# Full attention on one core: another order for TensorE inside each quarter of a head

## The reference, cut to what matters

```python
q = (hidden_states @ Wq.T + bq).reshape(b, s, HEADS, HEAD_DIM)
k = (hidden_states @ Wk.T + bk).reshape(b, s, HEADS, HEAD_DIM)
v = (hidden_states @ Wv.T + bv).reshape(b, s, HEADS, HEAD_DIM)
q = q * SCALE
scores = jnp.einsum('bqhd,bkhd->bhqk', q, k)
probs = jax.nn.softmax(scores.astype(jnp.float32), axis=-1).astype(scores.dtype)
out = jnp.einsum('bhqk,bkhd->bqhd', probs, v).reshape(b, s, d)
```

## Time and profile before

| | us |
|---|---|
| median of 3 runs (lowest to highest) | 3234.82 (3233.41 to 3235.3) |
| the profiled execution's own time | 3234.58 |
| its span, first to last instruction | 3232.9 |
| mean granted TensorE clock over the span | 0.934 |
| PE busy / DVE busy / ACT busy | 2513.5 / 2434.3 / 1832.9 |

### The profile page before, as it was taken

The page is one execution under the profiler, slowest core; times in us unless marked ns, Lnnn a source line. Parts: engine busy times, 40 slices in busy tenths (PEclk is TensorE's granted clock), DMA queues, the critical chain, the costliest instruction groups (busy, mean ns, idle before and its releaser), DMA issues. The chain is left out here.

```text
span 3232.9 us, 47502 instructions
## 1 busy us (share of the span) xinstructions
PE 2513.5 (78%) x12729; PEld 1044.9 (32%) x12911; DVE 2434.3 (75%) x4025; ACT 1832.9 (57%) x3590; POOL 1223.4 (38%) x1651
## 2 busy tenths in 40 slices
PE   5797799999999698799999999696745555555575
PEld 4543222222222443233333333284521010101454
DVE  6667788888886566777777777264279999999833
ACT  1212588888888111255555555303239999999521
POOL 1014533333331213378888888703550000000154
PEclk9899899999999699899999999887979999999688
DMA  3001322222221302712222222352131111110012
GB/s 94 1 1 62 100 79 71 78 71 78 71 79 54 95 1 77 252 61 80 81 83 77 73 80 68 107 211 60 40 109 40 33 32 32 33 33 26 18 45 81
DMA packets 192110, 223.46 MB, mean 69 GB/s; under 512 B 55152, under 2 KB 120944, under 8 KB 191472
## 3 DMA queue, kind: packets, MB, share of 16 engines
q1 hardware_dynamic: 152256, 192.41, 18.4%
q0 software_dynamic: 29696, 23.27, 3.1%
q10 hardware_dynamic: 9968, 5.51, 0.6%
HBM read 136.67 MB, written 83.76 MB: 68 GB/s over the span
## 5 line engine op out<-in xcount | busy, mean ns | idle before, releaser
L1253 DVE TENSOR_REDUCE neg_max<-ps 128x1 f32<-128x1024 f32 x512 | 602.5, 1219 | 93.8 <-PE ps L1147 87.0
L1632 POOL TENSOR_TENSOR acc<-acc,prob 128x512 f32<-128x512 f32 (+3 forms) x640 | 577.8, 943 | 87.5 <-PE ps L1481 87.5
L1226 ACT ACTIVATE prob<-ps 128x512 f32<-128x512 f32 x1024 | 556.3, 601 | 88.1 <-PE ps L1161 74.8
L2071 DVE TENSOR_REDUCE neg_max<-ps 128x1 f32<-128x1024 f32 x512 | 579.3, 1210 | 3.2 <-PE ps L2057 3.2
L2093 ACT ACTIVATE ps<-ps,neg_max 128x1024 f32<-128x1024 f32 x512 | 557.2, 1088 | 0.3 <-DVE neg_max L2071 0.3
L2057 PE MATMUL ps<-k_stack,q_stack 128*128 128x512 bf16 x992 | 303.5, 386 | 277.1 <-ACT ps L2093 273.9
L1561 ACT ACTIVATE prob<-ps 128x512 f32<-128x512 f32 (+3 forms) x640 | 266.5, 477 | 247.9 <-PE ps L1465 122.1
L1602 DVE TENSOR_REDUCE neg_max<-ps 128x1 f32<-128x128 f32 (+7 forms) x512 | 388.0, 758 | 17.5
L1161 PE MATMUL ps<-q_stack,k_stack 128*128 128x512 bf16 x946 | 292.8, 386 | 6.8 <-ACT prob L1226 4.6
L1171 PE MATMUL ps<-prob,v 128*32 128x512 f32 x2048 | 280.9, 620 | 3.7 <-ACT prob L1226 0.7
L1600 DVE TENSOR_TENSOR ps<-ps,mask_qk 128x128 f32<-128x128 f32 x512 | 151.1, 295 | 148.3 <-PE ps L1438 144.8
(11 more groups left out here) (304 smaller groups left out, 3820.0 us busy)
## 6 DMA issues: line engine op xcount, KB each, us to landing
q_stack<-q_parts SPq DMA_DIRECT2D x576, 48.0 KB
k_stack<-k_parts SPq DMA_DIRECT2D x576, 48.0 KB
o_quads<-o_out SPq DMA_DIRECT2D x64, 256.0 KB
v<-v_wide SPq DMA_DIRECT2D x32, 512.0 KB
o_pairs<-o_out SPq DMA_DIRECT2D x64, 256.0 KB, 6.2
num<-o_pairs SPq DMA_DIRECT2D x8, 2048.0 KB
q_parts<-parts SPq DMA_DIRECT2D x24, 384.0 KB, 2.7
k_parts<-parts SPq DMA_DIRECT2D x24, 384.0 KB, 2.7
```

The costliest lines, as they stand in the source:

```text
L1226: nc.scalar.activation(prob[:, m % RING, :], ps[:, bank(m), :], ACT.Exp).then_inc(exped.sem, 1)
L1253: nc.vector.tensor_reduce(neg_max[:, i.slot(2), m:m + 1], ps[:, first:first + 2, :].rearrange("p b n -> p (b n)"), AX.X, ALU.max, negate=T ...
L1632: nc.gpsimd.tensor_tensor(sums, sums, weights(j, u, h), ALU.add).then_inc(added.sem, 1)
L2071: nc.vector.tensor_reduce(neg_max[:, i.slot(2), qt:qt + 1], ps[:, 2 * (qt % 4):2 * (qt % 4) + 2, :], AX.XY, ALU.max, negate=True).then_inc ...
```

## The change

The order of TensorE in each group becomes: first pass `2g`, second score `4g`, first pass `2g + 1`, second scores `4g + 1` and `4g + 2`, prob by v of the group before, second score `4g + 3`. The transpose of the maxima moves from the end of group 1 to group 0, between prob by v and the last second score, and ACT's copy of it from behind the eighth exponential to behind the third. The rotation of banks is written as a list of 17 turns for each head; since 17 is no multiple of 3, a head starts on another bank than the one before it, where before each head started on bank 4. The waits for banks follow from that list.

```diff
-    TURN = NT // 2
+    turns = [0, 1, 2, "max"] + list(range(3, NT))
...
+    def bank(what, c):
+
+        return S2 + (len(turns) * c + turns.index(what)) % RING2
+
+    def wait_for_bank(pe, what, c):
+
+        at = len(turns) * c + turns.index(what) - RING2
+        while at >= -len(turns):
+            j, user = divmod(at, len(turns))
+            user = turns[user]
+            if user == "max" and 0 <= j + 1 < HEADS:
+                m_read.wait(pe, j + 1)
+                return
+            if user != "max" and 0 <= j < HEADS:
+                exped.wait(pe, j * NT + user)
+                return
+            at -= RING2
...
                 for g in range(4):
+                    if one:
+                        first_pass(i, 2 * g)
                     if two:
-                        for m in range(4 * g, 4 * g + 3):
-                            second_scores(j, m, there(n, 1))
+                        second_scores(j, 4 * g)
+                    if one:
+                        first_pass(i, 2 * g + 1)
+                    if two:
+                        second_scores(j, 4 * g + 1)
+                        second_scores(j, 4 * g + 2)
                     if g > 0 and two:
                         weigh(j, g - 1)
                     if g == 0 and there(n, 3):
                         weigh(i - 3, 3)
+                    if g == 0 and there(n, 1):
+                        turn_shift(i - 1)
                     if two:
-                        second_scores(j, 4 * g + 3, there(n, 1))
-                    if one:
-                        first_pass(i, 2 * g)
-                        first_pass(i, 2 * g + 1)
-                    if g == 1 and there(n, 1):
-                        turn_shift(i - 1, j if two else None)
+                        second_scores(j, 4 * g + 3)
...
-                    if g == 0 and there(n, 3):
+                    if m == 3 and there(n, 3):
                         read_output(i - 3, n)
-                    if g == 1 and there(n, 1):
+                    if m == 2 and there(n, 1):
                         h = i - 1
                         m_mm.wait(act, h.times(1))
```

More of the change, by code:

```diff
@@ L1148, in first_pass, with second_scores @@
                                  k_low[i.slot(2)][low, :], start=True, stop=True).then_inc(s1_mm.sem, 1)
-            def second_scores(j, n, turned):
+            def second_scores(j, n):
                 kt, c = tiles[n]
[L1153 to L1161, removed]
+                wait_for_bank(pe, n, j.c)
+                nc.tensor.matmul(ps[:, bank(n, j.c), :], ks[j.slot(4)][:, kt * P:(kt + 1) * P],
                                  qs[j.slot(4)][:, c * GROUP:(c + 1) * GROUP], start=True,
@@ L1172, in weigh, with turn_shift @@
                                      start=kt < 2, stop=kt >= KTS - 2).then_inc(pv_mm.sem, 1)
-            def turn_shift(h, j):
+            def turn_shift(h):
                 split.wait(pe, h.times(1))
                 m_read.wait(pe, h.times(1, -1))
-                if j is not None:
-                    exped.wait(pe, j.times(NT, TURN - RING2))
-                nc.tensor.transpose(ps[0:SHIFT * KTS, MAX_BANK, 0:P // 2].bitcast(BF16),
+                wait_for_bank(pe, "max", h.c - 1)
+                nc.tensor.transpose(ps[0:SHIFT * KTS, bank("max", h.c - 1), 0:P // 2].bitcast(BF16),
                                     shift[:, h.slot(2), :], S.ident_b[:]).then_inc(m_mm.sem, 1)
@@ L1220, in step @@
                 j = i - 2
[L1221 to L1227, removed]
-                    if g == 0 and there(n, 3):
+                for m in range(NT):
+                    if there(n, 2):
+                        s2_mm.wait(act, j.times(NT, m))
+                        pv_mm.wait(act, j.times(NT, m - RING))
+                        nc.scalar.activation(prob[:, m % RING, :], ps[:, bank(m, j.c), :],
+                                             ACT.Exp).then_inc(exped.sem, 1)
+                    if m == 3 and there(n, 3):
                         read_output(i - 3, n)
-                    if g == 1 and there(n, 1):
+                    if m == 2 and there(n, 1):
                         h = i - 1
@@ L1236, in step @@
                         nc.scalar.activation(shift_rows[0:SHIFT * KTS, h.slot(2), :],
-                                             ps[0:SHIFT * KTS, MAX_BANK, 0:P // 2].bitcast(BF16),
+                                             ps[0:SHIFT * KTS, bank("max", h.c - 1), 0:P // 2].bitcast(BF16),
                                              ACT.Copy).then_inc(m_read.sem, 1)
```

## The result

The changed kernel takes 3275.61 us (median of 4 runs, 3271.91 to 3276.79) against 3234.11 us for the kernel before, measured beside it: 1.0128 times the time, with a 95% interval of 1.0114 to 1.0142. It is 1.3% slower. The profiled execution has a span of 3274.4 us, 41.5 more than before. Forecast were 3274 us and a range of 3265 to 3289.

What follows compares the result with a forecast made beforehand. TensorE was taken to bound the kernel, setting a head's length. From the profiled 3234.58 us, +44.6 - 3.1 - 3 + 0.5 = +39.0 gave 3273.6, forecast as 3274 us; range 3265 to 3289.

Steps and rivals of the forecast that it cites:

- part 2: DVE's reductions: their loop takes 2.64 us a group, like TensorE; spacing first passes removes 0.05 us lateness a head, -3.1 us.
- rival 2: DVE's loop, 2.63 us, sets the group; TensorE's 0.1 us are disguised waits for it; 69 us less, 3165; chance 2%.
- Part 1: First passes taken apart on TensorE: two more changes of shape, +0.18 us for each group, +44.6 us, or +49.6.
- Part 3: Transpose moved between prob by v and a second score: no difference or 6.2 us gained; the middle taken, -3 us.
- part 5: Ends of the attention: at the start TensorE waits once or twice for reductions, +0.5 us, with 0 to 1.
- Part 4: ACT and the banks: both copies fall in the first group, yet prob by v needn't wait; 0.2 us left.
- Rival 3: ACT's crowded first group makes prob by v wait for the output copy; 0.3 us lost each head, 3293; chance 13%.
- Rival 1: Extra changes of shape hidden beside running matmuls; a group stays 2.64 us, -3 to -9 us, about 3228; chance 5%.

Runs made afterwards that it cites:

- e6_transpose_late: The changed kernel with the transpose of the maxima behind group 0's last second score; one execution, 3329.21 us beside 3276.83 for the kernel before.
- e1_paired: The changed kernel with each group's two first passes next to each other again, at the group's start; 3226.02 us beside 3232.55 for the kernel before.
- e5_half_split: The changed kernel with first passes taken apart only in groups 0 and 2, paired in 1 and 3; 3249.85 us, 1.0051 times the kernel before.

## Why the prediction was right

**TensorE bounds, and the changes of shape are the price.** Right, and shown: the loss is there with 64-row matmuls and gone with 72-row ones, in the same order. That the changed kernel's distances on TensorE are the same in every head agrees with it. One reading under it was wrong: the 8.3 us of waits are missing records, and the only wait there was, for DVE in the late group, is not among them. It changes nothing in the sum, which takes the late group from the distances. (The loop of part 2 comes to 2.64; rival 2 quotes it as 2.63.)

**Part 1, +0.18 us for each group: right in kind, a sixth too small.** The four steps between first pass and second score measure 0.32 each, where I had taken 0.31 for the step out of a first pass, from the second pass of a pair in the earlier trace rows. A first pass that itself follows a change keeps 0.32; that is 0.022 of the 0.033 us missing in each group, and the rest is the rounding of the rows to 0.01. From the starts in the trace, in thousandths: 0.322 and 0.003 + 0.319 for the way in and out, twice, then 0.226, 0.309 and 1.028: 2.851 us for a group, against 0.322 + 0.226 + 0.311 + 0.226 + 0.216 + 0.309 + 1.028 = 2.638 before. 0.213 x 248 = 52.8 us, instead of the 44.6 in the sum and 49.6 at its end.

**Part 2, -3.1 us: right.** The late group is gone; the head of the kernel before with half of DVE's work is 0.059 shorter, 62 x 0.059 = 3.7 us.

**Part 3, -3 us: the size was off, and made up for part 1.** From the last records of prob by v to the transpose is 0.409 us and on to the second score 0.152, against 0.525 directly: 0.036. Before, it was 0.309 + 0.155 - 0.311 = 0.153, with the 0.309 from the kernel with half of DVE's work (0.320 - 0.309 belongs to the late group, part 2). So 62 x 0.117 = 7.3 us came back. The distance from prob by v to the transpose is that of the answer without a change of shape (-6.2 us), and my middle between two possible answers was neither.
**Sum.** 52.8 - 3.7 - 7.3 = 41.8, where the heads measure 41.6, the attention as a whole 41.7 (753.2 us from its first matmul to its last one's end, 711.5 before) and the span 41.5. So of the ends (part 5, +0.5) next to nothing is seen. The forecast of 39.0 was 8.2 too low in part 1 and 4.3 too high in part 3. That it came within 3 us of the measured time is in part luck, since the two errors have opposite signs; either of them alone would have left the time in the range (3270 or 3282).

**Part 4, no wait for ACT: right.** Prob by v started 708.24 - 707.92 = 0.32 after the output copy, where 0.25 was worked out (4.4 - 4.15). Rival 3 did not come. How near it is shows in the kernel with the late transpose, where the other order of the two copies made a wait at once, of a second score for the rows' copy and not of prob by v for the output.

**Rival 1 (the changes are hidden)** fell with the trace after: no load was pulled ahead over a change of shape. In the trace's starts all loads between a first pass and a second score come 0.004 to 0.005 us ahead of their matmul, where between two second scores the load comes 0.216 ahead. **Rival 2 (DVE's loop)** fell twice, with the halved reductions: 5 us instead of 60, and 0.02 us for a head with paired first passes. The nearness of the loop's 2.64 to TensorE's 2.64 was what spoke for it, and it means only that both were level.

## What to carry to other kernels

Where matmuls of different array shapes alternate on a full TensorE, count the changes of shape in the order, not only the matmuls: here each cost 0.09 to 0.11 us, half a 512-column matmul, and evening out another engine's supply at the price of more changes loses if that engine isn't the bound. Put short matmuls of narrow shape next to others of the same shape (the transpose behind prob by v cost 0.04 instead of 0.15). And before relieving an engine whose loop is as long as the bound, halve its work once and see what a step gains: here 0.06 of 10.78 us. Before trusting a wait of the profile, compare the counts of weight loads and matmuls of its line: here all 40 waits of TensorE were missing records.

## What the runs showed of the hardware that was not expected

- 72 rows with 128 columns count as the full array: 0.22 to 0.23 us to and from a 128-row matmul in both 72-row kernels. Two matmuls of 64 rows side by side start 0.003 us apart, and take 0.22 together.
- A first pass between two second scores pays 0.011 us more on its way out than the second of a pair (0.322 against 0.311 from its own start). The same 0.010 or 0.011 stands behind every matmul that itself comes late, behind a change of shape or behind a wait: a second score behind another shape is followed by the next second score after 0.226, that one by the third after 0.216; the transpose behind the late pair came after 0.320, and after 0.309 where DVE was not late; behind the second score that waits in `e6_transpose_late`, prob by v came after 0.320 instead of 0.309; and the first pair of a head in `e1_paired` takes 0.236 and 0.322, but 0.226 and 0.312 with half of DVE's work. So a short wait of TensorE costs 0.01 us more than itself. Why, no run shows.
- The transpose starts 0.409 us after the last record of prob by v, 0.116 earlier than a second score there (0.525). That is a little more than a change of shape costs.
- In the changed kernel DVE's first reduction of a head starts 704.35 - 703.85 = 0.50 us after its matmul, 0.06 later than the 0.44 of the next group, just when POOL's second operation ends. That is not the cause: in `e5_half_split` the reduction starts 0.50 after its matmul too (710.75 and 710.25), and POOL's second operation only at 710.76. The first reduction of a head is the one that has a second wait ahead of it in DVE's program (`split.wait`); no run took that wait out. It costs nothing, as DVE has room there.
